# Gated networks of a four-layer model: four batches in one written-out block instead of two passes of an engine loop

## The chip, the cores and the metric

The kernel runs on one core of a Trainium2 chip. The metric is device time in microseconds (us) of the whole kernel; the kernel before takes 6068.03 us, the median of three runs (6062.26 to 6073.97). The engines named below are TensorE (PE in the profile; PEld is its weight load), VectorE (DVE), ScalarE (ACT), GpSimd (POOL) and SyncE (SP). Each has its own stream of instructions and waits on semaphores.

## The reference

Four layers, each an attention-like part and a feed-forward part, both wrapped in a layer norm, a modulation and a gated residual. The input is 4 sequences ("batches") of 512 tokens with 256 features. Three of the four feed-forward parts are gated networks, and only these are touched:

```python
def _mlp(x, w1, w2, w3):                 # layer 0: 16 experts of 176, one shared of 352
    a = jnp.dot(x, w1.T); b = jnp.dot(x, w3.T)
    return jnp.dot((jax.nn.silu(a) * b), w2.T)
y = shared(x) + sum_e share[e] * _mlp(x, w1[e], w2[e], w3[e])

gate = silu(qlinear(x, wq_gate, s_gate)) # layer 1: 704 hidden, integer weights and scales
out = qlinear(gate * qlinear(x, wq_up, s_up), wq_down, s_down)

hidden = fwht(silu(x @ W1.T) * (x @ W3.T))   # layer 3: 1024 hidden, Hadamard transform
out = hidden @ W2.T

x = x + gb * out                         # all of them: gated residual
```

## The kernel before

The kernel is a row of stages. The residual stream `x_res` stays on the chip through all of them. A stage is made of blocks: a block gives each engine a list of instructions, and all engines meet at its end. `ph.clear()` resets the stage's semaphores and lets all engines meet once more.

The gated networks are computed transposed: a hidden tile is 128 hidden features by the 512 tokens of one batch. For each tile, TensorE computes the two up projections into two banks, ScalarE applies silu, VectorE multiplies, and TensorE adds the tile's down projection into two banks that collect the batch's output. After the last tile of a batch `add_gated` (lines 328 to 339) lets VectorE multiply the two banks by the gate (L333) and add them to `x_res` (L339).

- `gated_mlp` serves layer 1 (`qmlp_run`, 6 tiles per batch) and layer 3 (`hmlp_run`, 8 tiles per batch), in float32. TensorE is one tile ahead: the ups of tile n (L1809), then the down of tile n-1 (L1529). The two batches of a pass collect in different banks.
- `expert_mlp` serves layer 0 (`moe_mlp`, 25 tiles per batch), in bfloat16 with each float32 value split into three parts. Each tile has 12 up matmuls (L1793), one that spreads the expert shares (L1799) and 12 downs (L1605). TensorE is two tiles ahead, and the two batches of a pass collect in the same two banks, so the first down of the second batch waits until VectorE has read the banks (`pe.wait_ge(tmp_s, 2)`).

Around both stands a loop on the engines, `with nc.Fori(0, NB - 1, 2) as b`, whose body handles the batches b and b+1. It runs twice. At the end of each pass all engines drain, `add_gated` runs for the second batch, `ph.clear()` resets the semaphores, so that counts begin at zero again, and all engines branch back. The batch number is a register, so that addresses with it are worked out on the engines by the instructions that the lists below call ISA and REGISTER_ALU.

Two other stages have loops of this kind, with one batch a pass and several blocks in a pass: `latent_attention` (4 passes, behind the expert stage) and `low_rank_update` (4 passes, behind the quantised stage).

Of the kernel before, what the change touches and what calls it, by code (L numbers as in the profile page):

```python
# [13 lines left out]
ALU = mybir.AluOpType  # L14
ACT = mybir.ActivationFunctionType
# [5 lines left out]
P = 128  # L21
# [1469 lines left out]

def seq(t, b):

    return t[:, :, bass.ds(b, 1), :].rearrange("p k o n -> p k (o n)")


def gated_mlp(k, tag, tiles, up, w2, silu_scale=None, up_scale=None):


    nc = k.nc  # L1500
    with Phase(nc, tag) as ph:
        sl = ph.sb("silu", [P, 2, S])
        hid = ph.sb("hid", [P, 2, S])
        tmp = ph.sb("tmp", [P, 2, 2, D])
        up_s, silu_s, hid_s, down_s = (ph.sem(n) for n in ("up", "silu", "hid", "down"))
        tmp_s, out_s = ph.sem("tmp"), ph.sem("out")
        bank = k.bank

        pair = 2 * tiles
        down_bank = lambda n, i: bank[6 + i if n < tiles else 4 + i]  # L1510

        with nc.Fori(0, NB - 1, 2) as b:
            with nc.Block() as block:  # L1513

                @block.tensor
                def _(pe):
                    for n in range(pair + 1):
                        if n < pair:
                            m, own = n % tiles, b + n // tiles
                            after(pe, hid_s, n - 1)  # L1520
                            last = up(pe, bank[n % 2], 0, m, own)
                            last = up(pe, bank[2 + n % 2], 1, m, own)
                            last.then_inc(up_s, 1)
                        if n:
                            m = (n - 1) % tiles
                            pe.wait_ge(hid_s, n)
                            for t in range(NC):

                                last = pe.matmul(down_bank(n - 1, t // 2)[:, (t % 2) * D:(t % 2 + 1) * D],  # L1529
                                                 hid[:, (n - 1) % 2, t * P:(t + 1) * P], w2[:, m, :],  # L1530
                                                 start=(m == 0 and t % 2 == 0), stop=(m == tiles - 1 and t % 2 == 1),
                                                 skip_group_check=True)
                            last.then_inc(down_s, 1)

                @block.scalar
                def _(act):
                    for n in range(pair):
                        m = n % tiles
                        act.wait_ge(up_s, n + 1)
                        after(act, hid_s, n - 1)  # L1540
                        sc = silu_scale[:, m:m + 1] if silu_scale is not None else 1.0
                        act.activation(sl[:, n % 2, :], bank[n % 2][:, :], ACT.Silu, scale=sc).then_inc(silu_s, 1)

                @block.vector
                def _(dve):
                    for n in range(pair):
                        m = n % tiles
                        dve.wait_ge(silu_s, n + 1)
                        after(dve, down_s, n - 1)
                        if up_scale is not None:  # L1550
                            dve.scalar_tensor_tensor(hid[:, n % 2, :], bank[2 + n % 2][:, :], up_scale[:, m:m + 1],
                                                     sl[:, n % 2, :], ALU.mult, ALU.mult).then_inc(hid_s, 1)
                        else:
                            dve.tensor_tensor(hid[:, n % 2, :], sl[:, n % 2, :], bank[2 + n % 2][:, :], ALU.mult)\
                                .then_inc(hid_s, 1)
                        if n == tiles:
                            dve.wait_ge(down_s, tiles)
                            add_gated(dve, k, 1, b, [down_bank(0, i) for i in range(2)], tmp, tmp_s, out_s, 0)
                    dve.wait_ge(down_s, pair)
                    dve.wait_ge(out_s, 2)  # L1560
                    add_gated(dve, k, 1, b + 1, [down_bank(tiles, i) for i in range(2)], tmp, tmp_s, out_s, 2)

            ph.clear()


def expert_mlp(k, tag, tiles, up, shares, w2):
# [4 lines left out]
    with Phase(nc, tag) as ph:  # L1571
# [7 lines left out]
        high_s, rest_s, mid_s, low_s = (ph.sem(n) for n in ("high", "rest", "mid", "low"))  # L1579
        tmp_s, out_s = ph.sem("tmp"), ph.sem("out")  # L1580
        bank = k.bank
        pair = 2 * tiles
        slot = lambda n: parts[:, n % (LAG + 1)]

        with nc.Fori(0, NB - 1, 2) as b:
            with nc.Block() as block:

                @block.tensor
                def _(pe):
                    for n in range(pair + LAG):  # L1590
                        if n < pair:
                            m, own = n % tiles, b + n // tiles
                            after(pe, hid_s, n - 1)
                            up(pe, bank[n % 2], 0, m, own)
                            up(pe, bank[2 + n % 2], 1, m, own)
                            shares(pe, bank[4 + n % 2], m, own).then_inc(up_s, 1)
                        if n >= LAG:
                            d = n - LAG
                            m = d % tiles
                            pe.wait_ge(low_s, d + 1)  # L1600
                            if d == tiles:
                                pe.wait_ge(tmp_s, 2)
                            for t in range(NC):
                                for i in range(3):
                                    last = pe.matmul(bank[6 + t // 2][:, (t % 2) * D:(t % 2 + 1) * D],  # L1605
                                                     slot(d)[:, i, t * P:(t + 1) * P], w2[:, m, :],
                                                     start=(m == 0 and t % 2 == 0 and i == 0),
                                                     stop=(m == tiles - 1 and t % 2 == 1 and i == 2), skip_group_check=True)
                            last.then_inc(down_s, 1)

                @block.scalar
                def _(act):
                    def high(n):
                        act.wait_ge(hid_s, n + 1)
                        after(act, down_s, n - LAG)
                        act.activation(slot(n)[:, 0, :], hid[:, n % 2, :], ACT.Copy).then_inc(high_s, 1)

                    def middle(n):
                        act.wait_ge(rest_s, n + 1)
                        act.activation(slot(n)[:, 1, :], rest[:, n % 2, :], ACT.Copy).then_inc(mid_s, 1)  # L1620

                    for n in range(pair + 1):
                        if n < pair:
                            act.wait_ge(up_s, n + 1)
                            after(act, prod_s, n - 1)
                            act.activation(sl[:, n % 2, :], bank[n % 2][:, :], ACT.Silu).then_inc(silu_s, 1)
                        if n:
                            middle(n - 1)
                        if n < pair:
                            high(n)  # L1630

                @block.vector
                def _(dve):
                    def remainder(n):
                        dve.wait_ge(high_s, n + 1)
                        after(dve, low_s, n - 1)
                        dve.tensor_tensor(rest[:, n % 2, :], hid[:, n % 2, :], slot(n)[:, 0, :], ALU.subtract).then_inc(rest_s, 1)

                    def lowest(n):
                        dve.wait_ge(mid_s, n + 1)  # L1640
                        dve.tensor_tensor(slot(n)[:, 2, :], rest[:, n % 2, :], slot(n)[:, 1, :], ALU.subtract).then_inc(low_s, 1)

                    for n in range(pair + 1):
                        if n < pair:
                            dve.wait_ge(silu_s, n + 1)
                            dve.tensor_tensor(pr[:, n % 2, :], sl[:, n % 2, :], bank[2 + n % 2][:, :], ALU.mult)\
                                .then_inc(prod_s, 1)
                            dve.wait_ge(prod_s, n + 1)
                            after(dve, rest_s, n - 1)
                            dve.tensor_tensor(hid[:, n % 2, :], pr[:, n % 2, :], bank[4 + n % 2][:, :], ALU.mult)\  # L1650
                                .then_inc(hid_s, 1)
                        if n:
                            lowest(n - 1)
                        if n < pair:
                            remainder(n)
                        if n == tiles + 1:
                            dve.wait_ge(down_s, tiles)
                            add_gated(dve, k, 1, b, [bank[6], bank[7]], tmp, tmp_s, out_s, 0)
                    dve.wait_ge(down_s, pair)
                    dve.wait_ge(out_s, 2)  # L1660
                    add_gated(dve, k, 1, b + 1, [bank[6], bank[7]], tmp, tmp_s, out_s, 2)

            ph.clear()


def experts(k):
# [1747 lines left out]
```

## Time and profile before

| what | value |
|---|---|
| time, median of three runs | 6068.03 us (6062.26 to 6073.97) |
| the profiled execution's own time | 6062.66 us |
| its span, first to last instruction | 6060.9 us |
| mean granted TensorE clock | 0.930 |
| PE busy | 5218.4 us (86%) |
| DVE busy | 3477.9 us (57%) |
| ACT busy | 3055.4 us (50%) |
| expert network, first up matmul to last add | 3443.30 to 3877.34 us |
| quantised network | 4581.15 to 4716.50 us |
| Hadamard network | 5876.27 to 6052.05 us |

Times in the trace are us from the start of the span. A row of the timeline gives the start, the length, the engine, the line, and in square brackets how long the engine had been idle and what ended it. Consecutive like instructions are merged into one row with their count. Of a float32 matmul in the program two records stand in the trace. TensorE's granted clock is a share of full speed, 2.4 GHz: 1.00 is that level, 0.50 the level of 1.2 GHz.

### The profile page before, as it was taken

The page shows a single profiled execution, that of the slowest core. Times are in us where ns is not written, and L with a number is a line of the kernel's source. Part 1 is how long each engine was busy: PE and PEld are TensorE (multiplying, and loading weights), DVE is VectorE, ACT ScalarE, POOL GpSimd, SP SyncE. Part 2 cuts the span into 40 slices and gives each one's busy share as a digit, 9 for nine tenths or more (in the row PEclk, how much of TensorE's full clock was granted, in tenths as well). Part 3 has the DMA queues.
Part 4 walks back from the last instruction along what each step waited for, and adds up shares of the span by engine and source line. Part 5 has one row for each costly group of instructions (what it writes and reads, how often), then busy time and mean ns, then how long its engine had stood idle before and what let it go on. Part 6 is the DMA issues. An engine that isn't in the chain of part 4 may idle for free. (4 is left out here: it accounts for less than half of the span.)

```text
span 6060.9 us, 92111 instructions
## 1 busy us (share of the span) xinstructions
PE 5218.4 (86%) x32318; PEld 3888.8 (64%) x32318; DVE 3477.9 (57%) x6531; ACT 3055.4 (50%) x8926; POOL 1176.6 (19%) x1352
## 2 busy tenths in 40 slices
PE   5799999999989999899999699899998597399968
PEld 4587777877877778777877555555555354255545
DVE  4576766666766667666666566555552554543331
ACT  2466666666666666666666343344441243325421
POOL 0222222322222222222222000011110321002210
PEclk7799999999999999999999799899999798688879
DMA  2000000000000000000000100100000100000000
GB/s 92 11 19 17 15 20 19 18 13 17 19 19 17 13 18 22 17 15 17 18 18 17 42 1 1 65 1 0 0 0 20 27 1 13 21 1 1 1 21 14
DMA packets 51088, 103.50 MB, mean 17 GB/s; under 512 B 12848, under 2 KB 20176, under 8 KB 49520
## 3 DMA queue, kind: packets, MB, share of 16 engines
q1 hardware_dynamic: 50672, 98.07, 5.4%
q8 instruction: 248, 4.06, 0.3%
q14 instruction: 168, 1.38, 0.1%
HBM read 90.43 MB, written 5.52 MB: 16 GB/s over the span
## 5 line engine op out<-in xcount | busy, mean ns | idle before, releaser
L896 ACT ACTIVATE dh_pb<-bank 64x128 f32<-64x128 f32 x3072 | 829.1, 270 | 273.9 <-PE bank L670 240.3
L684 PE MATMUL bank<-dh_cw,dh_pb 128*128 128x128 f32 x5120 | 701.6, 281 | 112.4 <-ACT dh_pb L896 111.0
L684 PEld LDWEIGHTS bank<-dh_cw,dh_pb 128*128 128x128 f32 x5120 | 635.9, 193 | 190.4 <-ACT dh_pb L896 163.7
L1034 DVE SCALAR_TENSOR_TENSOR dh_kq<-bank,dh_conv_kq,dh_kq 128x511 f32<-128x511 f32 (+2 forms) x408 | 305.4, 749 | 184.5 <-ACT dh_kq L853 173.3
L902 ACT ACTIVATE dh_cw<-bank 128x256 f32<-128x256 f32 x640 | 244.5, 384 | 255.3 <-PE bank L684 248.0
L621 PE MATMUL bank<-hT,dh_w_kq 128*128 128x512 f32 x544 | 276.7, 633 | 82.9 <-DVE dh_kq L1034 75.3
L1034 DVE SCALAR_TENSOR_TENSOR dh_v<-bank,dh_conv_v,dh_v 128x511 f32<-128x511 f32 (+2 forms) x384 | 284.0, 746 | 91.3 <-ACT dh_v L853 82.2
L1793 PE MATMUL bank<-moe_h_split,moe_w 128*128 x1200 | 280.2, 384 | 22.5 <-PEq L89 14.9
L633 PE MATMUL bank<-dh_w_vz,hT 128*128 128x256 f32 x1024 | 245.5, 383 | 22.0 <-ACT dh_zs L864 22.0
L1128 DVE TENSOR_TENSOR dh_zz<-dh_zz,bank 128x512 f32<-128x512 f32 x130 | 89.1, 686 | 283.1 <-PE bank L597 281.1
L621 PE MATMUL bank<-hT,dh_w_vz 128*128 128x512 f32 x512 | 242.5, 596 | 8.4 <-DVE dh_v L1034 8.4
L1105 DVE TENSOR_TENSOR dh_cw<-dh_cw,bank 128x256 f32<-128x256 f32 x512 | 206.5, 412 | 73.3 <-ACT dh_cw L902 73.3
L1267 POOL TENSOR_TENSOR dh_ntoff<-dh_kkm,dh_et 64x256 f32<-64x256 f32 x128 | 91.9, 723 | 782.9 <-PE bank L597 782.9
L759 PE MATMUL bank<-dh_wo_gated,dh_ww 128*128 128x256 f32 x1040 | 236.3, 380 | 0.0
L301 POOL TENSOR_TENSOR ln_rstd<-ln_var_eps,nhalf 128x16 f32<-128x16 f32 x8 | 23.2, 2903 | 1064.2 <-DVE ln_var_eps L291 1064.2
L2884 PE MATMUL bank<-blk_queries,blk_keys 32*128 32x384 f32 (+3 forms) x1024 | 195.8, 523 | 30.1 <-ACT blk_att_e L3013 19.9
L633 PEld LDWEIGHTS bank<-dh_w_vz,hT 128*128 128x128 f32 x1024 | 184.5, 190 | 54.6 <-ACT dh_zs L864 34.8
L1275 POOL TENSOR_TENSOR dh_pto<-dh_qkm,dh_et 128x512 f32<-128x512 f32 x128 | 163.2, 1275 | 285.6 <-PE bank L597 285.5
L1259 POOL TENSOR_TENSOR dh_inj<-ident,dh_R 128x512 f32<-128x512 f32 x130 | 176.3, 1376 | 206.8 <-DVE dh_et L1086 124.8
L1793 PEld LDWEIGHTS bank<-moe_h_split,moe_w 128*128 128x128 bf16 x1200 | 118.6, 99 | 147.5 <-issue 29.1
L670 PE MATMUL bank<-ident,dh_cw 128*128 128x128 f32 x1280 | 200.3, 275 | 10.9 <-ACT dh_cw L902 10.9
L759 PEld LDWEIGHTS bank<-dh_wo_gated,dh_ww 128*128 128x128 f32 x1040 | 193.3, 191 | 24.0 <-ACT dh_ww L929 0.2
(416 smaller groups left out, 12134.4 us busy)
## 6 DMA issues: line engine op xcount, KB each, us to landing
dh_rates<-delta_rates SPq DMA_DIRECT2D x130, 256.0 KB, 3.6
dh_w_vz<-in_L_wvz SPq DMA_DIRECT2D x17, 512.0 KB, 3.5
mod_w<-in_L_wmod SPq DMA_DIRECT2D x4, 1536.0 KB, 7.5
dh_w_kq<-in_L_wkq SPq DMA_DIRECT2D x18, 256.0 KB, 2.6
dh_wo<-in_L_wo SPq DMA_DIRECT2D x16, 256.0 KB, 4.2
moe_w<-in_L_w13T SPq DMA_DIRECT2D x1, 3200.0 KB, 16.6
later_gates<-mod_gate SPq DMA_DIRECT2D x3, 1024.0 KB, 4.0
gate<-later_gates SPq DMA_DIRECT2D x6, 512.0 KB, 3.5
```

The source lines that it names most:

```text
L621: last = pe.matmul(pj_bank(n), w[:, kk, :], k.hT[:, kk, n % NB, :], start=(kk == 0), stop=(kk == KD - 1))
L633: last = pe.matmul(bank[PJ_B][:, i * D:(i + 1) * D], k.hT[:, kk, 2 * (m % 2) + i, m // 2 * P:(m // 2 + 1) * P], wvz[:, kk, RPH * DH:], sta ...
L670: last = pe.transpose(bank[TURN][:, (2 * j + g) * P:(2 * j + g + 1) * P], src[:, 0, 2 * g:2 * g + 2, :].rearrange("p b n -> p (b n)"), k.i ...
L684: last = pe.matmul(square(j)[:, b, :, :], pb[j][:, b, :], src[:, :, b, :], start=True, stop=True)
L759: last = pe.matmul(bank[OUT[b // 2]][:, (b % 2) * D:(b % 2 + 1) * D], ww[j][:, b, :], wob[:, j, b, :], start=(j == 0 and b % 2 == 0), stop ...
L896: last = act.activation(out[half, :, o, half], src[halves[o], :, half], ACT.Copy)
L902: act.activation(cw[j][:, 0, :, :], square(j)[:, :, 0, :], ACT.Copy).then_inc(h["a_c"], 1)
L1034: dve.scalar_tensor_tensor(y, pj_bank(n)[:, 0:S - i], taps(n)[:, TAPS - 1 - i:TAPS - i], y, ALU.mult, ALU.add).then_inc(s["v_cs" if i < TA ...
L1105: dve.tensor_tensor(cw[j][:, 1, :, :], old[:, 1, :, :], square(j)[:, :, 1, :], ALU.add).then_inc(h["v_c"], 1)
L1259: pool.tensor_tensor(inj[j][:, :, :], mask_bc(k.ident[:, :], NB), row_bc(R[:, next_par(t), j, next_chunk(t), :], P), ALU.mult).then_inc(hs ...
L1793: last = pe.matmul(bank[:, :], w13[:, kk, which, m * P:(m + 1) * P], seq(hs[:, j, :, :, :], b)[:, kk, :], start=(n == 0), stop=(n == 3 * K ...
L2884: last = pe.matmul(ring(u)[:, at:at + (NC - j) * P], keys[r, G, j * P:(j + 1) * P], queries[r, G, j * P:S], start=(at == 0), stop=(j == TU ...
```

## The change

Both functions lose the loop. One block holds all four batches, with a count of tiles n from 0 to NB * tiles - 1; the batch is n // tiles and now a number known when the program is built. Semaphores are no longer cleared between the second and third batch but go on counting, and the waits are written against the running counts. The body of each network becomes twice as long in instructions. Nothing is computed otherwise.

```diff
 def seq(t, b):
-    return t[:, :, bass.ds(b, 1), :].rearrange("p k o n -> p k (o n)")
+    return t[:, :, b, :] if isinstance(b, int) else t[:, :, bass.ds(b, 1), :].rearrange("p k o n -> p k (o n)")

 def gated_mlp(...):
-        pair = 2 * tiles
-        down_bank = lambda n, i: bank[6 + i if n < tiles else 4 + i]
-        with nc.Fori(0, NB - 1, 2) as b:
-            with nc.Block() as block:
+        every = NB * tiles
+        down_bank = lambda n, i: bank[(6 if n // tiles % 2 == 0 else 4) + i]
+        with nc.Block() as block:
                 def _(pe):
-                    for n in range(pair + 1):
-                            m, own = n % tiles, b + n // tiles
+                for n in range(every + 1):
+                        m, own = n % tiles, n // tiles
...
                         pe.wait_ge(hid_s, n)
+                        if m == 0:
+                            after(pe, tmp_s, 2 * ((n - 1) // tiles - 1))
...
             def _(dve):
-                        if n == tiles:
-                            dve.wait_ge(down_s, tiles)
-                            add_gated(dve, k, 1, b, ..., tmp, tmp_s, out_s, 0)
-                    dve.wait_ge(down_s, pair)
-                    dve.wait_ge(out_s, 2)
-                    add_gated(dve, k, 1, b + 1, ..., tmp, tmp_s, out_s, 2)
+                def add(b):
+                    dve.wait_ge(down_s, tiles * (b + 1))
+                    after(dve, out_s, 2 * b)
+                    add_gated(dve, k, 1, b, [down_bank(tiles * b, i) for i in range(2)], tmp, tmp_s, out_s, 2 * b)
+                    if n % tiles == 0 and n:
+                        add(n // tiles - 1)
+                add(NB - 1)
-            ph.clear()
+        ph.clear()

 def expert_mlp(...):                      # the same, and:
-                            if d == tiles:
-                                pe.wait_ge(tmp_s, 2)
+                        if m == 0:
+                            after(pe, tmp_s, 2 * (d // tiles))
-                        if n == tiles + 1:
+                    if n % tiles == 1 and n > 1:
+                        add(n // tiles - 1)
```

What it moves, in TensorE's list of the expert network. Before, the end of the loop body (L1605 is the down projection; the 36 are the downs of the last three tiles, with no up matmuls left to stand between them):

```order
L1793 MATMUL bank<-moe_h_split,moe_w 128x512 x12
L1799 MATMUL bank<-moe_sharesT,moe_spread 128x512
L1605 MATMUL bank<-moe_w,moe_mlp_parts 128x256 x36
L1586 UNCONDITIONAL_BRANCH
L1585 REGISTER_ALU
L1585 COMPARE_AND_BRANCH
```

Now, at the same place (the 50th tile and the two behind it; lines are numbered anew):

```order
L1797 MATMUL bank<-moe_h_split,moe_w 128x512 x12
L1803 MATMUL bank<-moe_sharesT,moe_spread 128x512
L1607 MATMUL bank<-moe_w,moe_mlp_parts 128x256 x12
L1797 MATMUL bank<-moe_h_split,moe_w 128x512 x12
L1803 MATMUL bank<-moe_sharesT,moe_spread 128x512
L1607 MATMUL bank<-moe_w,moe_mlp_parts 128x256 x12
```

The third batch's up matmuls now stand between the second batch's last downs, as those of the second batch already did between the downs of the first.

On VectorE, the loop of the quantised network before (L1551 makes a hidden tile, L333 and L339 are `add_gated`; it is run twice, and the ISA rows work out addresses):

```order
L1551 SCALAR_TENSOR_TENSOR qmlp_run_hid<-bank,qmlp_s_hidden,qmlp_run_silu 128x512 x5
L333 ISA
L333 TENSOR_TENSOR qmlp_run_tmp<-bank,gate 128x512 x2
L339 ISA
L339 TENSOR_TENSOR x_res<-x_res,qmlp_run_tmp 128x512
L339 ISA
L339 TENSOR_TENSOR x_res<-x_res,qmlp_run_tmp 128x512
L1513 UNCONDITIONAL_BRANCH
L1512 REGISTER_ALU
L1512 COMPARE_AND_BRANCH
```

Now, between the second and the fourth batch:

```order
L1557 SCALAR_TENSOR_TENSOR qmlp_run_hid<-bank,qmlp_s_hidden,qmlp_run_silu 128x512 x6
L333 TENSOR_TENSOR qmlp_run_tmp<-bank,gate 128x512 x2
L339 TENSOR_TENSOR x_res<-x_res,qmlp_run_tmp 128x512 x2
L1557 SCALAR_TENSOR_TENSOR qmlp_run_hid<-bank,qmlp_s_hidden,qmlp_run_silu 128x512 x6
L333 TENSOR_TENSOR qmlp_run_tmp<-bank,gate 128x512 x2
L339 TENSOR_TENSOR x_res<-x_res,qmlp_run_tmp 128x512 x2
```

The adds of the second batch now stand behind the third batch's first hidden tile, and the branch is gone. At the start of the loop body TensorE also had 12 ISA and 2 REGISTER_ALU instructions in the expert network and 4 ISA in each of the others; none of these is left.

## Rows read from the trace of the kernel before

**Rows 1.** Windows, all engines: us, busy (count) by engine; PE clock, DMA share, GB/s.
```profile
4590.39:4641.99 51.60, 51.60 (x161) 30.40 (x160) 10.00 (x14) 6.87 (x10) 0.00 (x0) 1.00 0.00 0
4658.51:4710.11 51.60, 51.60 (x162) 30.40 (x161) 10.00 (x14) 6.87 (x10) 0.00 (x0) 1.00 0.00 0
3454.16:3640.54 186.38, 185.69 (x1127) 110.00 (x1126) 123.54 (x186) 79.19 (x136) 0.00 (x0) 1.00 0.00 1
```

**Rows 2.** Timeline, PE, expert network, where the first batch gives way to the second.
```profile
3557.37 0.38 PE L1799 MATMUL bank<-moe_sharesT,moe_spread 128*128 x1
3558.45 1.47 PE L1605 MATMUL bank<-moe_w,moe_mlp_parts 128*128 128x256 bf16 x12 [0.69 <-DVE moe_mlp_tmp L333]
...
3562.34 0.38 PE L1799 MATMUL bank<-moe_sharesT,moe_spread 128*128 x1
```

**Rows 3.** Timeline, PE, expert network, across the end of the loop's first pass.
```profile
3644.66 0.38 PE L1799 MATMUL bank<-moe_sharesT,moe_spread 128*128 x1
...
3648.77 0.38 PE L1799 MATMUL bank<-moe_sharesT,moe_spread 128*128 x1
...
3663.07 4.98 PE L1793 MATMUL bank<-moe_h_split,moe_w 128*128 x12 [7.53 <-issue]
...
3677.72 0.38 PE L1799 MATMUL bank<-moe_sharesT,moe_spread 128*128 x1
```

**Rows 4.** Timeline, same place: VectorE's last add, and ScalarE's first instruction after it.
```profile
3656.93 1.28 DVE L339 TENSOR_TENSOR x_res<-x_res,moe_mlp_tmp 128x512 f32 x2
3659.23 1.28 ACT L1626 ACT_TABLE_LOAD   x1 [5.95 <-PEq L89]
```

**Rows 5.** Windows, all engines: the matmuls behind that gap.
```profile
3663.07:3668.10 5.03, 5.03 (x13) 1.91 (x14) 0.00 (x0) 0.00 (x0) 0.00 (x0) 0.55 0.02 7
```

**Rows 6.** Timeline, PE, quantised network, where batches change inside a pass.
```profile
4616.19 1.89 PE L1529 MATMUL bank<-qmlp_dw,qmlp_run_hid 128*128 128x256 f32 x8
...
4621.35 1.89 PE L1529 MATMUL bank<-qmlp_dw,qmlp_run_hid 128*128 128x256 f32 x8
```

**Rows 7.** Timeline, quantised network, across the end of the first pass.
```profile
4641.99 3.72 PE L1529 MATMUL bank<-qmlp_dw,qmlp_run_hid 128*128 128x256 f32 x16
...
4647.10 1.28 DVE L339 TENSOR_TENSOR x_res<-x_res,qmlp_run_tmp 128x512 f32 x2
...
4649.85 8.83 PE L1809 MATMUL bank<-hT,qmlp_w 128*128 x16 [4.13 <-PEq L89]
...
4658.51 1.89 PE L1529 MATMUL bank<-qmlp_dw,qmlp_run_hid 128*128 128x256 f32 x8
```

**Rows 8.** Timeline, PE, Hadamard network, across the end of the first pass.
```profile
5957.03 3.62 PE L1529 MATMUL bank<-hmlp_dw,hmlp_run_hid 128*128 128x256 f32 x16
...
5964.99 8.69 PE L1809 MATMUL bank<-hT,hmlp_w 128*128 x16 [4.34 <-PEq L89]
...
5973.52 1.89 PE L1529 MATMUL bank<-hmlp_dw,hmlp_run_hid 128*128 128x256 f32 x8
```

**Rows 9.** Timeline, entry into the loops: the last instruction before, the first matmul.
```profile
3440.66 1.23 DVE L1786 CAST moe_h_split<-route_rest 128x2048 bf16<-128x2048 f32 x1
...
3443.30 5.30 PE L1793 MATMUL bank<-moe_h_split,moe_w 128*128 x12 [14.94 <-PEq L89]
...
4578.40 1.76 DVE L1843 TENSOR_TENSOR qmlp_dw<-qmlp_dw,qmlp_s_down 128x1536 f32<-128x1536 f32 x1
...
4581.15 9.41 PE L1809 MATMUL bank<-hT,qmlp_w 128*128 x16 [7.94 <-PEq L89]
```

**Rows 10.** Timeline, DVE, latent attention's loop: end of a pass, start of the next.
```profile
4080.22 1.28 DVE L339 TENSOR_TENSOR x_res<-x_res,mla_out_tmp 128x512 f32 x2
4082.72 0.69 DVE L2278 COPY mla_ht<-hT 128x1024 f32 x1 [1.22 <-PEq L89]
```

**Rows 11.** DMA queues, in the window 3454:3640: packets, MB, share of engines.
```profile
q8 instruction: 8, 0.13, 0.3%
q14 instruction: 4, 0.03, 0.1%
```

More of the change, by code:

```diff
@@ new lines, in gated_mlp, with _ @@
+        every = NB * tiles
+        down_bank = lambda n, i: bank[(6 if n // tiles % 2 == 0 else 4) + i]
+        with nc.Block() as block:
+            @block.tensor
+            def _(pe):
+                for n in range(every + 1):
+                    if n < every:
+                        m, own = n % tiles, n // tiles
+                        after(pe, hid_s, n - 1)
+                        last = up(pe, bank[n % 2], 0, m, own)
+                        last = up(pe, bank[2 + n % 2], 1, m, own)
+                        last.then_inc(up_s, 1)
+                    if n:
+                        m = (n - 1) % tiles
+                        pe.wait_ge(hid_s, n)
+                        if m == 0:
+                            after(pe, tmp_s, 2 * ((n - 1) // tiles - 1))
+                        for t in range(NC):
+                            last = pe.matmul(down_bank(n - 1, t // 2)[:, (t % 2) * D:(t % 2 + 1) * D],
+                                             hid[:, (n - 1) % 2, t * P:(t + 1) * P], w2[:, m, :],
+                                             start=(m == 0 and t % 2 == 0), stop=(m == tiles - 1 and t % 2 == 1),
+                                             skip_group_check=True)
+                        last.then_inc(down_s, 1)
+            @block.scalar
+            def _(act):
+                for n in range(every):
+                    m = n % tiles
+                    act.wait_ge(up_s, n + 1)
+                    after(act, hid_s, n - 1)
+                    sc = silu_scale[:, m:m + 1] if silu_scale is not None else 1.0
+                    act.activation(sl[:, n % 2, :], bank[n % 2][:, :], ACT.Silu, scale=sc).then_inc(silu_s, 1)
+            @block.vector
+            def _(dve):
+                def add(b):
+                    dve.wait_ge(down_s, tiles * (b + 1))
+                    after(dve, out_s, 2 * b)
+                    add_gated(dve, k, 1, b, [down_bank(tiles * b, i) for i in range(2)], tmp, tmp_s, out_s, 2 * b)
+                for n in range(every):
+                    m = n % tiles
+                    dve.wait_ge(silu_s, n + 1)
+                    after(dve, down_s, n - 1)
+                    if up_scale is not None:
+                        dve.scalar_tensor_tensor(hid[:, n % 2, :], bank[2 + n % 2][:, :], up_scale[:, m:m + 1],
+                                                 sl[:, n % 2, :], ALU.mult, ALU.mult).then_inc(hid_s, 1)
+                    else:
+                        dve.tensor_tensor(hid[:, n % 2, :], sl[:, n % 2, :], bank[2 + n % 2][:, :], ALU.mult)\
+                            .then_inc(hid_s, 1)
+                    if n % tiles == 0 and n:
+                        add(n // tiles - 1)
+                add(NB - 1)
@@ L1581, in expert_mlp @@
         bank = k.bank
-        pair = 2 * tiles
+        every = NB * tiles
         slot = lambda n: parts[:, n % (LAG + 1)]
[L1585 to L1600, printed above, removed]
-                            if d == tiles:
-                                pe.wait_ge(tmp_s, 2)
[L1603 to L1655, printed above, removed]
-                        if n == tiles + 1:
[L1657 to L1663, printed above, removed]
@@ L1666, in experts @@
+        ph.clear()
 def experts(k):
```

104 lines of the change are left out of this document (66 added, 38 removed).

## The prediction

> **What bounds the kernel now.** I read the page's busy times first: TensorE is busy for 5218.4 of 6060.9 us, so a stage is worth what TensorE's idle time in it is worth. Then I read windows inside the three gated networks. In ten tiles of the quantised network TensorE is busy for 51.60 of 51.60 us, in both passes, and in 45 tiles of the expert network for 185.69 of 186.38 us, at clock 1.00 [rows 1]. Inside a pass there is nothing to win. Third, the timeline at the end of the first pass. In the expert network TensorE sits idle for 7.53 us before the second pass's first matmul [rows 3], in the quantised one for 4.13 us [rows 7], in the Hadamard one for 4.34 us [rows 8]. These three gaps are the change's object. Last, the first rows of each stage, since the loop's entry goes too.
>
> One idle piece inside a pass matters, for the change repeats it: at the batch change TensorE waits 0.69 us for VectorE to read the two banks [rows 2].
>
> **Expert network, the loop's border.** I measure with the share matmul (L1799), one per tile. Its starts lie 3648.77 - 3644.66 = 4.11 us apart in steady work [rows 3]. Tile 49, the last of the first pass, has it at 3648.77; tile 53 at 3677.72, in steady work again. That is 28.95 us for four tiles. Written out, the border looks as the one inside the pass does, where tile 27 to tile 28 took 3562.34 - 3557.37 = 4.97 us instead of 4.11, that is 0.86 more, for the wait on the banks [rows 2]. So 4 x 4.11 + 0.86 = 17.30 us, and the gain is 28.95 - 17.30 = **11.65 us**. The difference holds everything at once: two downs of the first pass that no up matmul covered, the last add, the clearing and the branch, TensorE's late start, the slow clock behind it (0.55 [rows 5], so mostly the level of 1.2 GHz after 7.53 us of idling, and 4.98 us for twelve matmuls), and two tiles of fill. The 0.86 is the term that the change adds: one more wait for VectorE. Queued behind it on TensorE are the down and the next tile's ups, and ScalarE's silu waits for those, so its whole length is on the path.
>
> Of that gap one part is not the meeting of the engines. VectorE's last add ends at 3656.93 + 1.28 = 3658.21, ScalarE starts at 3659.23, 1.02 us later, TensorE at 3663.07, 4.86 us later [rows 3, 4]. In the quantised network TensorE starts 4649.85 - 4648.38 = 1.47 us after the add [rows 7]. So the expert's TensorE loses another 3.84 us (4.86 - 1.02) to something of its own. I take it for the fetch of its instructions after the jump back over a long body (1250 matmuls against 96 in the quantised body). The Trainium skill (Runtime: NRT & Kernel Launch, Instruction fetch mechanics) says that fetching runs ahead only in sequence, that TensorE's buffer holds 2048 instructions, and that a branch to a target outside it must wait for a fetch; by that the expert's body does not fit and the other two do, and the trace agrees, 4.86 against 1.47 us.
>
> **Quantised network, the border.** The measure is the start of the second last down of a pass (4641.99) and of the next pass's first down (4658.51): 16.52 us for two tiles [rows 7]. In steady work, batch change included, a tile takes 4621.35 - 4616.19 = 5.16 us [rows 6]; the collecting banks alternate, so there is no wait for VectorE here, and after the change the third batch takes the first one's banks, whose add was done some 30 us before. 16.52 - 10.32 = **6.20 us**. What is late next is nothing but TensorE's own work.
>
> **Hadamard network, the border.** 5973.52 - 5957.03 = 16.49 us [rows 8], less 10.32 = **6.17 us**.
>
> **Moved work.** The adds of batches 1 are moved from an empty machine into the third batch's first tiles. They are two pairs of about 1.3 us on VectorE (1.28 a pair [rows 4]). VectorE is busy for 10.00 of 51.60 us in the quantised network and 123.54 of 186.38 in the expert one [rows 1]; in the first they hide wholly, as at the other batch changes; in the second their price is the 0.86 counted. If that cover were too thin, VectorE's four operations would cost 2.6 us at most, at one border.
>
> **Entries and ends.** TensorE's first matmul comes 3443.30 - 3441.89 = 1.41 us after VectorE's last result in the expert network and 4581.15 - 4580.16 = 0.99 us in the quantised one [rows 9]. The first has 10 address instructions more, which gives about 0.04 us for one; 22 of them go on TensorE at the entries, so about 0.9 us, and the loop's last comparison goes at three ends, some 0.1 us. I take **1.0 us**. Bounds: 0 (the block's meeting hides them all) and 3.4 us (1.41 + 0.99 + 0.99, everything between the stages gone, which can't be since the meeting stays).
>
> **Sum.** 11.65 + 6.20 + 6.17 + 1.0 = **25.0 us**. The profiled execution took 6062.66 us, so it becomes 6037.7. That execution lies 5.4 us under the median of the runs shown; against 6068.03 the same gain gives **6043.0 us**, and that is what I predict, a gain of 0.41%. The gain alone has bounds of 24.0 - 2.6 = 21.4 and 24.0 + 3.4 = 27.4. Runs of one kernel spread over 12 us, so the likeliest case's own range is 6034 to 6052.
>
> **Rivals.**
>
> *Later loops lose what these win (no change).* The longer bodies push the code of latent attention and of the low-rank update to other places. They have three jumps back each, and today the jump costs nothing to see: VectorE restarts 4082.72 - 4081.50 = 1.22 us after its last add [rows 10], the meeting alone being 1.02. If a place were unlucky, each jump could cost the 3.84 us that the expert's jump does: three make 11.5 us, so 6054.5; all six make 23.0 us, so 6066, which is no change. For it: there is such a price in this trace. Against it: their bodies are short, and the loops behind the first one restart at once. 5 in 100 for a visible loss, half of it still faster. The Trainium skill (Runtime: NRT & Kernel Launch, Instruction fetch mechanics) says that the engines other than TensorE hold 32 KiB of instructions in two blocks of 16 KiB, so that it would depend on where a body starts in a block; by that rule the outcome is the 11.5 us of the one loop, or nothing. No run here shows those blocks.
>
> *Straight code is fetched late (slower).* Twice as much new code passes through TensorE in the second half of the networks, and the 3.84 us could come back at each packet of instructions that arrives late. In 186 us of the expert network 12 packets arrive [rows 11], so about 12 stand in its second half. Ten late ones cost 38.4 us, more than the gain: 6043 + 38.4 = 6081, slower. It decides from seven on (26.9 us). Against it: those 12 packets came while TensorE was busy for 185.69 of 186.38 us, and the missing 0.69 is the wait of rows 2. The quantised network's first pass, with its code fetched for the first time, was as full as its second, 51.60 us each [rows 1]. 2 in 100.
>
> *The idle time is only moved.* The added wait at the third batch could be longer than its model, since semaphores now count on and the order of VectorE's work at the border is new. If the drain of the expert network (two downs with waits, 7.53 us of idling) came back by half, the gain would be 25 - 3.8 = 21.2 us: 6046.8. Against it: the border inside the pass has word for word the same order and costs 0.86. 8 in 100, inside the range.
>
> *The clock does not hold.* TensorE would run for some 420 us of the expert network with no rest. If its clock dropped to 1.2 GHz for 10 us at some place, 5 us of gain would go: 6048. Against it: 1.00 over 186 us [rows 1]. 3 in 100.
>
> **How the numbers follow.** The likeliest case, gain 21 to 28 us, has 82 in 100, the four rivals 5, 2, 8 and 3. A measurement of this kernel can tell about 0.2% (12 us) from no change. Faster by more: all of the first case, of the third and fourth rivals, and half of the first rival, less what the spread of the runs spoils (the case's end at 6052 is still 16 under): 0.93. Within 0.2%: 0.05. Slower: 0.02. The range reaches from 6034, the full gain in a low median, to 6055, which takes in three late jumps.
>
> **What would show it.** Right: in the profile after, TensorE's idle time at the third batch of the expert network is one wait of about 0.7 us on VectorE's L333 (clock 1.00 throughout), the share matmuls there are 4.97 us apart once, and the downs of the other two networks stay at 5.16 us; one table load on ScalarE per network instead of two; the first matmul of each network about 0.3 us (expert 0.6) nearer to the stage before. The expert network from its first matmul to its last add shrinks from 434.0 to about 422.4 us, the quantised from 135.4 to 129.2, the Hadamard from 175.8 to 169.6. Wrong: VectorE's restart in latent attention over 2 us after its add; TensorE idle in straight code with no releaser; or a clock under 1.00 inside the expert network.

## The result, and the profile after

The change takes 6047.19 us (median of 7 runs, 6037.01 to 6051.62), the kernel before 6068.45 us (7 runs, 6062.26 to 6074.06). The ratio is 0.9963, with a 95% interval of 0.9954 to 0.9972. That is 21.3 us by the medians and 17 to 28 us by the interval, where 25.0 us and 6043.0 us had been predicted.

The profiled execution took 6048.28 us, with a span of 6046.2 us. The head of its page, with the lines of the busy times and of the instruction queues:

```profile
span 6046.2 us, 91895 instructions
PE 5221.5 (86%) x32318; PEld 3893.8 (64%) x32318; DVE 3480.2 (58%) x6531; ACT 3055.8 (51%) x8923; POOL 1178.3 (19%) x1352
...
q8 instruction: 250, 4.10, 0.3%
q14 instruction: 172, 1.41, 0.1%
```

TensorE does the same work, and about as many instruction packets arrive as before (248 and 168). Three activations are gone, the second table load of each network.

TensorE's timeline at the third batch of the expert network (L1803 is the share matmul, L1607 the down), which answers to [rows 2, 3]:

```profile
3657.72 0.38 PE L1803 MATMUL bank<-moe_sharesT,moe_spread 128*128 128x512 bf16 x1
...
3670.07 0.38 PE L1803 MATMUL bank<-moe_sharesT,moe_spread 128*128 128x512 bf16 x1
3671.14 1.47 PE L1607 MATMUL bank<-moe_w,moe_mlp_parts 128*128 128x256 bf16 x12 [0.69 <-DVE moe_mlp_tmp L333]
...
3675.04 0.38 PE L1803 MATMUL bank<-moe_sharesT,moe_spread 128*128 128x512 bf16 x1
```

The gap of 7.53 us is gone. In its place stands the batch change of [rows 2], with the same wait of 0.69 us for L333 and 3675.04 - 3670.07 = 4.97 us from share matmul to share matmul. The first row is tile 49, the last one tile 53: by the prediction's own measure the border takes 3675.04 - 3657.72 = 17.32 us, where it took 28.95 and 17.30 had been worked out. The downs of the other two networks stay 5.16 us apart across the border, so that its two tiles take 10.32 us there.

Windows over the inside of the quantised and of the expert network (columns as in [rows 1]):

```profile
4588.05:4697.00 108.95, 108.95 (x340) 64.38 (x339) 23.23 (x33) 14.81 (x22) 0.00 (x0) 1.00 0.00 1
3460.00:3860.00 400.00, 397.92 (x2412) 235.53 (x2410) 266.06 (x401) 170.23 (x292) 0.00 (x0) 1.00 0.00 1
```

The quantised network has no idle time across its batch changes. In 400 us of the expert network TensorE idles for 2.08 us, three times 0.69. The clock is 1.00 in both.

The timeline of entries and ends, which answers to [rows 9]: VectorE's last work and TensorE's first matmul for two networks, and between them the last add of the expert network and the layer norm behind it.

```profile
3451.04 1.23 DVE L1790 CAST moe_h_split<-route_rest 128x2048 bf16<-128x2048 f32 x1
...
3453.36 3.87 PE L1797 MATMUL bank<-moe_h_split,moe_w 128*128 128x512 bf16 x9 [14.61 <-PEq L89]
...
3873.24 1.28 DVE L339 TENSOR_TENSOR x_res<-x_res,moe_mlp_tmp 128x512 f32<-128x512 f32 x2
3875.25 5.33 DVE L286 BATCH_NORM_STATS2 ln_stats<-x_res 128x6 f32<-128x256 f32 x16 [0.73 <-PEq L89]
...
4576.48 1.76 DVE L1847 TENSOR_TENSOR qmlp_dw<-qmlp_dw,qmlp_s_down 128x1536 f32<-128x1536 f32 x1
...
4578.89 9.32 PE L1813 MATMUL bank<-hT,qmlp_w 128*128 128x512 f32 x16 [7.26 <-PEq L89]
```

TensorE starts 3453.36 - 3452.27 = 1.09 us after VectorE's result instead of 1.41, and 0.65 instead of 0.99 us. The layer norm starts 0.73 us after the last add, where it was 0.90.

First matmul to last add of each network in us, by all the traces in which the network has that form (the experiments are told below; the fifth has another form of the expert network and is left out there). Behind them stand the differences of the means and what had been predicted:

| network | with the loop | written out | difference of the means | predicted |
|---|---|---|---|---|
| expert | 434.0, 432.2, 433.9 | 421.2, 420.7, 421.2, 420.8, 422.3, 420.8 | 12.3 | 11.65 |
| quantised | 135.4, 134.9, 134.9 | 128.9, 129.2, 129.2, 129.3, 128.9, 128.9, 128.9 | 6.0 | 6.20 |
| Hadamard | 175.8, 175.8, 175.7 | 169.6 (seven times) | 6.2 | 6.17 |
| entries and ends, first traces | | | 1.6 | 1.0 |

The quantised and the Hadamard network gave what the border alone should give. The expert network gave 0.6 us more, and that is not the border: its first tile, before any border, runs at a clock that differs from trace to trace. From the first matmul to the second share matmul it takes 8.27, 7.14 and 8.17 us in the three traces with the loop, and 6.68 to 8.32 in the six written out, 0.7 us less by the means. The granted clock over that stretch was 0.65 in the first trace of before and 0.75 in that of the change.

Together 26.1 us. The first two traces differ by only 14.7 us in span, since the profiled execution of the change lost 10.1 us ahead of the expert network, in code that is the same: 3453.36 against 3443.30 [rows 9]. Seven of them arise in the modulations, the stage behind the setup. Windows of that stretch, in the change and in a second execution of the kernel before (the first has clock 0.86 there):

```profile
20.00:90.00 70.00, 58.31 (x256) 51.66 (x256) 33.17 (x75) 14.45 (x33) 0.00 (x0) 0.79 0.30 112
```
```profile
20.00:90.00 70.00, 51.44 (x275) 46.96 (x276) 40.41 (x109) 16.16 (x36) 2.90 (x1) 0.88 0.29 111
```

### The profile page after: what moved, and what is told of

Same layout as the page of the kernel before. It is cut to its first block and busy times, and to the rows that moved or that the text cites. A ratio compares the mean times of both kernels' runs of the same rounds, so it can differ in the third digit from the quotient of the medians.

```text
span 6046.2 us, 91895 instructions
## 1 busy us (share of the span) xinstructions
PE 5221.5 (86%) x32318; PEld 3893.8 (64%) x32318; DVE 3480.2 (58%) x6531; ACT 3055.8 (51%) x8923; POOL 1178.3 (19%) x1352
## 3 DMA queue, kind: packets, MB, share of 16 engines
q14 instruction: 172, 1.41, 0.1%
## 5 line engine op out<-in xcount | busy, mean ns | idle before, releaser
L1797 PE MATMUL bank<-moe_h_split,moe_w 128*128 128x512 bf16 x1200 | 277.1, 381 | 14.6 <-PEq L89 14.6
L621 PEld LDWEIGHTS bank<-hT,dh_w_kq 128*128 128x128 f32 x544 | 96.1, 197 | 175.5 <-DVE dh_kq L1034 98.7
```

The lines of the kernel that those rows point to most:

```text
L621: last = pe.matmul(pj_bank(n), w[:, kk, :], k.hT[:, kk, n % NB, :], start=(kk == 0), stop=(kk == KD - 1))
L1797: last = pe.matmul(bank[:, :], w13[:, kk, which, m * P:(m + 1) * P], seq(hs[:, j, :, :, :], b)[:, kk, :], start=(n == 0), stop=(n == 3 * K ...
```

## The experiments

All ratios are to the kernel before.

**1 and 2. One network, or the other two.** The first kernel takes `expert_mlp` of the change and `gated_mlp` of before, the second the reverse.

> Only the expert network is written out in one block; the quantised and the Hadamard network keep the loop. Theory (each loop border costs TensorE its drain, the meeting, its late start and the slow clock behind it, and the three borders are independent): the expert network from its first matmul to its last add takes 421 to 422.5 us instead of 434.0, the other two stay at 135.4 and 175.8; with entry and end about 13 us less than before in all, ratio to before about 0.998. Rival (the written-out code shifts later loops to worse places): latent attention or the low-rank update is 3.8 us longer per jump back, 11 us or more in all, and the gain is gone.

> Only the quantised and the Hadamard network are written out; the expert network keeps its loop. Theory: the quantised network takes 129 instead of 135.4 us, the Hadamard one 169.6 instead of 175.8, the expert network stays at 434.0; in all about 13.5 us less than before, ratio about 0.998; e1 and e2 together give the whole gain. Rival (part of the gain needs both, or is given back elsewhere): the two gains do not add up to the 27 us that the networks with their entries and ends show in the profile of the change.

Measured: 0.9979 (0.9970 to 0.9988) and 0.9980 (0.9971 to 0.9989). In the first the expert network takes 421.2 us and the others 134.9 and 175.7; in the second 433.9, 129.2 and 169.6. The two gains of 0.21% and 0.20% add up to the 0.37% of the whole within their intervals. The borders are independent, as the theory has it.

**3. Two blocks without a loop.** Both functions of the kernel before, with this in each (and `seq` as in the change, since `b` is now a plain number):

```diff
-        with nc.Fori(0, NB - 1, 2) as b:
+        for b in range(0, NB, 2):
```

> The two passes of each network stand written out one behind the other, each with its own block, its drain, its clearing of semaphores and its meeting of the engines; only the jump back and the address instructions are gone. Theory (the expert network's TensorE loses 3.84 us of its gap to the fetch of its instructions after the jump back, the other two do not): TensorE's first matmul of the second pass comes 0.7 to 1.5 us after the last add in all three networks, instead of 4.86, 1.47 and 1.8 us; the expert network takes about 430 us (4 less than before), the quantised about 134.6, the Hadamard about 175; the rest of the gain (about 8 of 11.65 us, 5.5 of 6.2 twice) is not there. Whole kernel 7 to 8 us faster than before. Rival (the late start is the meeting and the clearing of semaphores themselves): TensorE still starts 4.9 us after the last add in the expert network, and the kernel gains under 3 us.

Measured: 0.9981 (0.9972 to 0.9990), 11.5 us, more than the 7 to 8 expected. The networks take 427.4, 132.8 and 174.6 us, where 430, 134.6 and 175 were expected. Its timeline at the border of the expert network, VectorE and then TensorE:

```profile
3661.22 1.28 DVE L339 TENSOR_TENSOR x_res<-x_res,moe_mlp_tmp 128x512 f32<-128x512 f32 x2
```
```profile
3658.49 1.48 PE L1605 MATMUL bank<-moe_w,moe_mlp_parts 128*128 128x256 bf16 x12 [0.69 <-DVE moe_mlp_parts L1641]
3663.23 2.75 PE L1793 MATMUL bank<-moe_h_split,moe_w 128*128 128x512 bf16 x12 [3.25 <-PEq L89]
...
5961.54 8.80 PE L1809 MATMUL bank<-hT,hmlp_w 128*128 128x512 f32 x16 [3.25 <-PEq L89]
```

The last row is the Hadamard network's border. In the expert network TensorE starts 3663.23 - 3662.50 = 0.73 us after the last add, with the meeting and the clearing still there. So 4.13 of the 4.86 us of late start [rows 3, 4] were the jump back with its address instructions; the rival is out. The other two networks start 0.96 and 0.72 us after the add. The part that I had not expected stands in the same row: twelve matmuls take 2.75 us, not 4.98. Windows behind the borders of the expert and the Hadamard network:

```profile
3663.23:3668.50 5.27, 5.27 (x25) 2.44 (x26) 1.37 (x2) 0.80 (x2) 0.00 (x0) 1.00 0.00 0
...
5961.54:5970.00 8.46, 8.46 (x16) 3.70 (x17) 0.69 (x1) 0.60 (x1) 0.00 (x0) 0.80 0.00 0
```

After 3.25 us of idling the clock had stayed at 1.00 in the expert network, and fallen in the Hadamard one, also after 3.25 us. Before its idling TensorE had been busy without a break in the Hadamard network, and with two breaks of 1.42 and 0.69 us in the expert one.

From tile 49 to tile 53 the expert network takes 22.44 us here. Of the 28.95 - 22.44 = 6.5 us won at that border, 4.1 are late start and 2.2 (4.98 - 2.75) are clock. The other two borders give 2.4 and 1.0 us, and the entries and ends about as much as in the change, 1.6 us; that makes the 11.5. The expectation had left out the clock, the entries and the ends. The 5.1 us that still part the expert's border from the change (22.44 - 17.32) I put down to the drain, the add, the meeting and the fill; no run takes them apart.

**4. One batch a pass.** The loops of the kernel before, with

```diff
-        with nc.Fori(0, NB - 1, 2) as b:
+        with nc.Fori(0, NB) as b:
...
-        pair = 2 * tiles
+        pair = tiles
```

and one `add_gated` a pass.

> The loops stay, but with one batch a pass: four passes and three jumps back instead of one in each network, and the bodies half as long (625 matmuls in the expert body instead of 1250). Theory (the expert's late start comes from the length of the body that is jumped over): TensorE restarts 1.0 to 1.6 us after the last add at all borders, the expert's too; the border costs about 9 us there and 6.2 us in the other networks, so the expert network is about 13 us longer than before, the other two 12.4 us each, the kernel about 38 us slower than before (6106). Rival (any jump back costs the expert's TensorE 4.86 us, whatever the length): its border costs 12.5 us, the expert network is 23 us longer, the kernel 48 us slower.

Measured: 1.0072 (1.0058 to 1.0086), 44 us slower, between the two expectations (38 and 48). The profile parts them. VectorE's and TensorE's timeline at the expert network's first border:

```profile
3561.47 1.28 DVE L339 TENSOR_TENSOR x_res<-x_res,moe_mlp_tmp 128x512 f32 x2
```
```profile
3564.14 5.30 PE L1791 MATMUL bank<-moe_h_split,moe_w 128*128 x12 [4.04 <-PEq L89]
```

TensorE restarts 3564.14 - 3562.75 = 1.39 us after the add, and 1.35 and 1.33 us at the other two borders, and the expert network is 13.1 us longer (447.1), the number of the theory. So a jump back as such does not cost 4.86 us; it did over the body of two batches. The half body also lies at another place, and no run parts length from place on TensorE. By the Trainium skill (Runtime: NRT & Kernel Launch, Instruction fetch mechanics), TensorE's buffer of 2048 instructions holds this body (625 matmuls and as many weight loads) and not the one of two batches. The trace agrees in sign.

The fetch itself can be seen in the DMA view, which counts packets of instructions. Between the last add and TensorE's restart at the expert's border, in the kernel before (window 3658.3:3663) and in experiment 3 (window 3662.6:3663.2):

```profile
q8 instruction: 1, 0.02, 1.7%
```
```profile
DMA packets 0, 0.00 MB, mean 0 GB/s; under 512 B 0, under 2 KB 0, under 8 KB 0
```

One packet of 16 KiB arrives in that gap in each of the three traces with the loop over two batches, where TensorE restarts 4.70 to 4.95 us after the add; none arrives at this run's three borders, nor at that of experiment 3. The trace does not name the engine that a packet is for.

The quantised and the Hadamard network are 10.6 and 12.2 us longer, near the 12.4 expected. The rest of the 44 us was in latent attention. Here is VectorE's timeline at its first border; its code is untouched:

```profile
4106.25 1.28 DVE L339 TENSOR_TENSOR x_res<-x_res,mla_out_tmp 128x512 f32 x2
4111.40 0.69 DVE L2276 COPY mla_ht<-hT 128x1024 f32 x1 [3.87 <-issue]
```

The wait was 1.22 us before. The three borders now take 3.87, 3.66 and 3.86 us, together 11.4 instead of 3.6, so 7.8 us are lost, and 13.1 + 10.6 + 12.2 + 7.8 = 43.7 us. That is the prediction's first rival, a later loop brought to a bad place, in another kernel than the one it was said of.

**5. Banks read early.** The change, with `add_gated` in two parts at the expert network's batch changes:

```diff
+                    border = n % tiles == 1 and n > 1
+                    if border:
+                        gated(n // tiles - 1)      # L333 twice
                     if n:
                         lowest(n - 1)
                     if n < every:
                         remainder(n)
-                    if n % tiles == 1 and n > 1:
-                        add(n // tiles - 1)
+                    if border:
+                        added(n // tiles - 1)      # L339 twice
```

> The change, and in the expert network VectorE reads the two collecting banks (L333) right behind the hidden tile, before it makes the lowest part of the previous tile, instead of after the whole tile. Theory (at a batch change TensorE waits for L333 alone, 0.69 us idle and 0.86 us in all): the wait shrinks to almost nothing, 0.6 to 0.8 us are won at each of three batch changes, the expert network takes about 419 instead of 421.1 us; the kernel is 2 us faster than the change, which its time can't show. Rival (the lowest part, now 1.3 us later, becomes the wait): the network stays at 421 us or grows.

Measured: 0.9959 (0.9945 to 0.9973). VectorE's and TensorE's timeline at the third batch (L1640 reads the banks):

```profile
3663.62 1.28 DVE L1640 TENSOR_TENSOR moe_mlp_tmp<-bank,gate 128x512 f32<-128x512 f32 x2
```
```profile
3665.37 0.38 PE L1815 MATMUL bank<-moe_sharesT,moe_spread 128*128 128x512 bf16 x1
3665.58 1.47 PE L1607 MATMUL bank<-moe_w,moe_mlp_parts 128*128 128x256 bf16 x12
```

The banks are read at 3664.90, before the down wants them, and the wait is gone. The share matmuls at the three batch changes are 4.12 us apart, as in steady work, so 3 x 0.86 = 2.6 us are won. The expert network takes 418.2 us, 2.9 less than in the change and the shortest of all the kernels. The time of the whole kernel can't be told apart from that of the change.

**6 to 8. Moving latent attention's code.** Experiment 4 left open whether the place of the loop or something else of that kernel cost it the 7.8 us in latent attention. These kernels are the change with 64, 176 or 256 one-element memsets on VectorE in the block before the loop, where it waits for 30 us:

```diff
+            pad = p2.sb("pad", [P, 64])
             with nc.Block() as block:
+
+                @block.vector
+                def _(dve):
+                    for i in range(64):
+                        dve.memset(pad[:, i:i + 1], 0.0)
```

> The change, and VectorE gets 64 memsets of one element a partition in the block before latent attention's loop, where it is idle for 30 us; they only shift the code behind them by 64 instructions. Theory (a jump back costs the fetch if the body lies unluckily; in the run with one batch a pass it cost VectorE 3.9 us three times in latent attention): shifted by 64 the body lies as unluckily as there, so VectorE restarts 3.9 us after the add at three borders instead of 1.2, latent attention is 8 to 12 us longer, the kernel as much slower than the change. Rival (that loss had to do with the shorter bodies elsewhere, or with ScalarE): latent attention takes as long as in the change, and the kernel too.

> As the one before, with 176 memsets instead of 64; they still fit into VectorE's idle 30 us. Theory of the place: this shift brings the body to a lucky place again (176 + 117 by my count is past a whole block of 256), so latent attention takes as long as in the change. Rival (more instructions ahead of the loop cost by their number): it is at least as much slower as with 64.

> As the two shifted kernels, with 256 memsets of one element. Shifts of 0 (the change) restart VectorE 1.2 us after the add at latent attention's borders, shifts of 64 and of 176 after 3.7 to 4.0 us. Theory (the place counts, in blocks of 256 instructions, and the body is longer than I had counted): a shift by exactly one block gives the place of the change back, so VectorE restarts after 1.2 us at all three borders and latent attention takes as long as in the change. Rival (any shift beyond some number costs, by the number of instructions ahead): it restarts after 3.7 to 4.0 us again, 7.5 to 8 us lost.

Measured: 0.9978 (0.9969 to 0.9987), 0.9977 (0.9968 to 0.9986) and 0.9957 (0.9944 to 0.9971). VectorE's timeline at the first border of latent attention, which answers to [rows 10], in the change and then shifted by 64, 176 and 256:

```profile
4078.72 1.28 DVE L339 TENSOR_TENSOR x_res<-x_res,mla_out_tmp 128x512 f32 x2
4081.24 0.69 DVE L2282 COPY mla_ht<-hT 128x1024 f32 x1 [1.24 <-PEq L89]
```
```profile
4067.86 1.28 DVE L339 TENSOR_TENSOR x_res<-x_res,mla_out_tmp 128x512 f32 x2
4072.85 0.69 DVE L2288 COPY mla_ht<-hT 128x1024 f32 x1 [3.71 <-issue]
```
```profile
4072.86 1.28 DVE L339 TENSOR_TENSOR x_res<-x_res,mla_out_tmp 128x512 f32 x2
4078.11 0.69 DVE L2288 COPY mla_ht<-hT 128x1024 f32 x1 [3.96 <-issue]
```
```profile
4074.00 1.28 DVE L339 TENSOR_TENSOR x_res<-x_res,mla_out_tmp 128x512 f32 x2
4076.51 0.69 DVE L2288 COPY mla_ht<-hT 128x1024 f32 x1 [1.24 <-PEq L89]
```

With 64 the loss is there as expected, if a little smaller: 3.71, 3.68 and 3.79 us at the three borders against 1.24, 1.20 and 1.19, so 7.5 us in three. With 176 my expectation failed; the loss is there too, 7.8 us. That left two readings, a place with a narrower lucky stretch than I had counted, or a plain number of instructions ahead. The kernel with 256 decides: it has the most instructions ahead and restarts after 1.24, 1.20 and 1.19 us. Experiment 4 had fewer instructions ahead than the kernel before and lost. So it is the place, and a shift by 256 VectorE instructions gives a good place back. This agrees with the blocks of 256 instructions of which the Trainium skill speaks (Runtime: NRT & Kernel Launch, Instruction fetch mechanics).

Here too the packets of instructions show the fetch. Between the add and VectorE's restart at the first border, with 64 (window 4069.2:4072.8) and with 256 (window 4075.3:4076.5):

```profile
q14 instruction: 1, 0.01, 0.5%
```
```profile
DMA packets 0, 0.00 MB, mean 0 GB/s; under 512 B 0, under 2 KB 0, under 8 KB 0
```

Exactly one such packet, of 8 KiB, arrives at each of the nine late restarts of latent attention (three each in experiments 4, 6 and 7), and none at the 27 prompt ones of the other nine traces. How wide the lucky stretch is stays open: shifts of 0 and 256 are in it, 64 and 176 not.

**9 and 10. Both kernels again, for second traces.**

> The kernel before once more, for a second trace of it. Theory (the stages ahead of the networks vary between executions of one program, with TensorE's clock in the modulations): the first layer norm starts between 75 and 87 us, not exactly at 79.6 as in the first trace, while the three networks repeat within 0.3 us: 434.0, 135.4 and 175.8 us. Rival (the 10 us that the change's profile lost ahead of the networks belong to the change): before repeats its 79.6 within 0.5 us.

> The change once more, for a second trace of it. Theory: the networks repeat 421.1, 128.9 and 169.6 us within 0.3 us, while the start of the first layer norm (86.6 us in the first trace) falls anywhere between 75 and 87 us. Rival: it starts at 86.6 us again, so the stages ahead of the networks are slower in the change.

Measured: spans of 6056.9 and 6038.8 us. The networks take 432.2, 134.9 and 175.8 us before and 420.7, 129.2 and 169.6 after; the expert network of before thus varies by 1.8 us and that of the change by 0.5, not by under 0.3. Of the 1.8 us, 1.1 are the clock in its first tile (8.27 against 7.14 us) and 0.7 the border (28.95 against 28.29). The first layer norm starts at 76.0 (before; first trace 79.6) and 83.4 us (change; 86.6). Over all twelve traces, with the same code in this stage, it starts between 75.8 and 86.6 us. The rival's strong form, a fixed start for each program, is out. Its weak form is not: each program came back within 3.6 us of itself and the change was later both times. The written-out expert network alone started at 75.8, so its longer code as such does not do it.

One thing stays unsettled. The two traces of before and those of experiments 1 and 2 reach the expert network between 3441.6 and 3443.3 us, the six with all three networks written out between 3444.5 and 3453.4, so later each time, by 5.5 us in the mean. But both traces of before come from executions faster than its median (6062.7 and 6058.6 against 6068.5 us), and experiments 3 and 4, at 3447.7 and 3451.7, fit neither group. Twelve traces don't tell a later start of this program from chance.

## Why the prediction was right

- *What bounds the kernel.* Right. TensorE had nothing to win inside a pass, and all of the gain that the traces locate is at the three borders, entries and ends.
- *Expert border, 11.65 us.* Right: 28.95 - 17.32 = 11.63 us by its own measure. The model of the new batch change held to the hundredth (4.97 us, 0.69 us of wait, three times). The 12.3 us of the whole network hold some 0.7 us more from the clock in its first tile, which changes from trace to trace. The border itself varies too: in the second trace of before it took 28.29 us, so a forecast from that trace would have been 0.65 us lower.
- *The 3.84 us of fetch inside it.* Right as a cause: 4.13 us went with the jump (experiment 3) and 3.5 with half the body (4.86 - 1.39, experiment 4), and a packet of instructions arrives in the gap at the late starts and at none of the prompt ones. The prediction took 1.02 us for the meeting alone; experiment 3 shows it with the clearing at 0.73, so a little more belongs to the jump. The clock, in the sum but not split off, is another 2.2 us at that border.
- *Quantised 6.20, Hadamard 6.17.* Right: 6.0 and 6.2 us by the whole networks, 16.5 to 10.32 us at both borders by the prediction's measure. No wait took the place of the removed ones, and the moved adds hid wholly.
- *Entries and ends, 1.0 us.* The mis-sized term: 1.6 us. The three entries gave 0.32, 0.34 and 0.33 us, 1.0 in all, where 0.9 had been put; but that is luck. The 0.9 was 22 address instructions at 0.04 us, most of them in the expert network, which was to start 0.6 us nearer and gave 0.32. With no address instruction left its entry is still 1.09 - 0.65 = 0.44 us slower than the quantised one's, so the 0.42 us from which the 0.04 was read had another cause, which stays open. The ends gave 0.6 us together, where I had put 0.1.
- *The sum.* 26.1 us in the networks with their entries and ends against 25.0; 0.6 to 0.7 us of the difference are the clock in the expert's first tile, 0.6 the entries and ends. The median moved by 21.3 us; the 3.7 us between forecast and median, and the 4.8 between traces and median, lie inside the interval of 17 to 28 us. Whether part of it is a stage ahead that runs later in this program is open, as told under experiments 9 and 10.
- *Rival "later loops lose".* It did not happen in this kernel (1.24 us against 1.22). As a mechanism it is real. Its price was too high: 2.5 to 2.7 us a jump in experiments 4, 6 and 7, not 3.84, so at most 8 us for the three jumps of latent attention, and the kernel would still have been faster. With a chance of 5 in 100 I had rated it too low: three of the eight kernels that moved this code fell into it (experiments 4, 6 and 7, two of them built to try it). The low-rank update never did: it restarts after 1.28 to 1.43 us in all twelve traces.
- *Rival "straight code is fetched late".* Out: 27 instruction packets arrived in 400 us of the expert network without any idle time but the three waits.
- *Rivals "idle time is moved" and "the clock does not hold".* Out, by the rows at the third batch and by the clock of 1.00 over 400 us.

## What to carry to other kernels

An engine loop's border costs the drain, the meeting, the restart of every engine and often a slow TensorE behind it; here 6.2 us with a short body and 11.6 with a long one. Where the body is a steady pipeline, write the passes out and let the semaphores count on; the batch change inside the pass shows beforehand what the border will cost. And when code grows or shrinks, look at the restart times of every loop behind it: its place alone made latent attention 7.5 to 7.8 us longer here, a third of what this change won.

## What the runs showed of the hardware that I had not expected

- A loop's jump back depends on where its body lies. On VectorE, latent attention restarts 1.2 us after its last add with shifts of 0 and 256 instructions, and 2.5 to 2.7 us later with 64 and 176.
- A late restart shows in the DMA view: one packet of instructions arrives in the wait, 8 KiB at the nine late restarts of latent attention and 16 KiB at the three of the expert network, and none at the prompt ones of these two.
- Idle times of equal length can leave TensorE at either clock: after 3.25 us it ran on at 1.00 at one border, and at 0.80 over the next 8.5 us at another.
- The modulations, early in the kernel, run at a mean granted clock between 0.79 and 0.88 from trace to trace, and end up to 10.8 us apart with the same code. Most of the spread of 12 to 16 us between runs of one kernel can come from there; that it does is not shown, since only the profiled runs have a trace.
